# Edge bias written by ScalarE and fewer groups in the tail, in a five-layer graph network on one core

## The chip, the cores and the metric

The kernel runs on one core of one Trainium2 chip. The metric is the device time of one execution in microseconds (us), as the median of several runs. Nothing is sharded, and no other core is used. PE is TensorE, DVE is VectorE, ACT is ScalarE, POOL is GpSimd, SP is SyncE.

## The reference

There are 12500 nodes with 64 features and 200000 edges with 32 attributes, sorted by destination. The destinations are dense at low node numbers (12500 times the square of a uniform number), the sources are uniform. Five layers run one after another:

```
h   = leaky(x @ W1 + b1) @ W2 + b2              # per node
e   = leaky(edge_attr @ We1 + be1) @ We2 + be2  # per edge, leaky slope 0.1
msg = h[src] * e * dot_scale                    # per edge
agg = segment_sum(msg, dst)                     # per node
out = x + agg * res_w
x   = layernorm(out) * ln_g + ln_b
```

Before the layers x is normalized and passed through a relu, and at the end the input is added. All is in float32. The change touches how `be2` is added to `e` and when a group of edges is worked on.

## The kernel before

The kernel is written engine by engine, each with its own program, ordered by semaphores alone. The first 1150 to 1240 us sort edges and prepare tables; they are not touched.

A layer then has two kinds of edge work. The first 101376 edges (dense destinations) lie in *slot groups*: 126 groups of 1024 slots, whose source rows are fetched in blocks and picked by a one-hot product on PE (`gathered`, line 1053, into `slot_ps`). The other edges lie in *gathered groups*: 97 groups of up to 1024 edges and one spill group (number 6), 98 in all. GpSimd fetches their source rows from `h_rows` by indirect DMA, 128 rows each (line 793), into a ring of nine buffers.

The loop has one slot group per step, 126 steps. Gathered groups are spread over them: `a_before(s)` counts the groups before step s, `a_at(s)` is the group whose message is made in step s, if any, and `b_at(s)` is the slot group. Before the change 92 gathered groups lie in the loop and six in the *tail*, six steps (126 to 131) with one group each. A chunk is 14 slot groups that add to the same nodes; the nine chunks have windows of 360, 328, 288, 248, 208, 168, 128, 88 and 48 columns, in this order.

In step s, each engine in its own order:

- PE: first edge product (`hidden_of`, line 976) for the groups of step s + 2, both kinds, into `hid_ps`; after the message of this step, the second edge product (`edge_out`, line 980) of the next gathered group into `e_ps`; after the slot message, that of the next slot group into `slot_ps`; window sums of this step's group (line 1016), which share a bank with the first `hid_ps` and so wait for the leaky operation of group s + 2; chunk sums (line 1029); then `gathered` for the next slot group (line 1053), which overwrites `slot_ps` once its contents were copied to `slot_e`.
- ACT: `hidden_tenth` (line 1252), 0.1 times the first product plus bias, for both kinds of step s + 2.
- DVE: the message product of the gathered group (line 1764, `msg_ready`), the slot product (line 1771, `slot_msg_ready`), the one-hot of the next group (line 1684), the leaky operation of both groups of step s + 2 (line 1676, `hid_acted`), the bias addition from `slot_ps` to `slot_e` and that within `e_ps` (line 1680), the addition of this step's window sums to the nodes (line 1732), then the one-hot for the next slot group (line 1684, up to 2880 columns).
- SP: after the message, the source indices of the group nine later (`load_src`), then attributes, picks and rows of later steps.

Node tiles (14 of 896 nodes) are finished as soon as all their edges are in. Each has a set of parts (`tile_parts`) hung into the middle or end of steps: centering, square, variance, root (line 1201), reciprocal (line 1618), affine (lines 1289 and 1291), then the two products of the next layer's h and its bias (line 1646, h_out). Eleven tiles lie in the loop, every ninth step, two in the tail (three steps each), and the last one follows in two pieces. The next layer's gathers wait until every tile's h is stored.

Of the kernel before, what the change touches and what calls it, by code (L numbers as in the profile page):

```python
# [11 lines left out]
P = 128  # L12
# [24 lines left out]
SPILL_AT = 6  # L37
# [7 lines left out]
TAIL_STEPS = 3  # L45
RECORD_BUFS = 6
# [23 lines left out]
def build(nc, a, N, D, E, ED, L):  # L70
# [19 lines left out]
    IN_LOOP = GA - TAIL_SLOTS * TAIL_STEPS  # L90
# [5 lines left out]
    def a_before(s):  # L96

        return -(-max(s, 0) * IN_LOOP // NB) if s <= NB else min(IN_LOOP + s - NB, GA)

# [48 lines left out]
    with ExitStack() as ctx:  # L148
# [187 lines left out]
        e_biased, slot_e_biased = sem("e_biased"), sem("slot_e_biased")  # L336
# [491 lines left out]
        def _(pe):  # L828
# [149 lines left out]
            def edge_out(acts, to):  # L978
                for j in range(TPH):
                    mm = pe.matmul(to[:, j * P:(j + 1) * P], acts[:, j * TILE:(j + 1) * TILE],  # L980
                                   w2s[:, :], start=True, stop=True)
                return mm

            def far_pass(l):
                with pe.Fori(0, NG) as g:
# [4 lines left out]
                    edge_out(hidden[:, 0, 0, :], e_ps).then_inc(far_e_ready, 1)  # L990
# [10 lines left out]
            def edges(l, last):  # L1001
                pe.wait_ge(edge_w_landed, 16 * (l + 1))
                pe.wait_ge(w2s_ready, 3 * (l + 1))
                pe.wait_ge(h_biased, 2 * (l + 1) * NT)
                own_wait(pe, "pe")

# [39 lines left out]
                def gathered(i):  # L1046
                    pe.wait_ge(source_pick_landed[i % 2], 16 * (l * (NB // 2) + i // 2 + 1))
                    pe.wait_ge(source_rows_landed[i % 2], 16 * (l * (NB // 2) + i // 2 + 1))
                    for k in range(TPG):
                        side, j = k % 2, k // 2  # L1050
                        for half in range(2):
# [3 lines left out]
                                           source_rows[0:ROWS, i % 2, k * D:(k + 1) * D], start=True, stop=True)  # L1055
# [3 lines left out]
                def step(s, part):  # L1059
# [15 lines left out]
                    if now == SPILL_AT:  # L1075
                        pe.wait_ge(spill_msg_ready, l + 1)
                    elif now is not None:
                        pe.wait_ge(msg_ready, l * GR + real(now) + 1)
                    if m is not None:
                        pe.wait_ge(hid_acted[0], l * GA + m + 1)  # L1080
                        edge_out(hidden[:, 0, m % 2, :], e_ps).then_inc(e_ready, 1)
                    k = b_at(s)
                    if k is not None:
                        pe.wait_ge(slot_msg_ready, l * NB + k + 1)
                    k = b_at(s + 1)
                    if k is not None:
                        pe.wait_ge(hid_acted[1], l * NB + k + 1)
                        edge_out(hidden[:, 1, k % 2, :], slot_ps).then_inc(slot_e_ready, 1)
                    if now is not None and now != SPILL_AT:
                        pe.wait_ge(hid_acted[0], l * GA + a_before(s + 3))  # L1090
                        window_sums(now)
                    if b_at(s) is not None:
                        if k is None:
                            own_wait(pe, "pe")
                        chunk_sums(s)
                    part("middle")
                    if k is not None:
                        pe.wait_ge(slot_e_biased, l * NB + k + 1)
# [91 lines left out]
        def _(act):  # L1190
# [68 lines left out]
            def edges(l, last):  # L1259
                k = l + 1  # L1260
                act.wait_ge(w2s_ready, 3 * (l + 1))
                own_wait(act, "act")

                def step(s, part):
# [667 lines left out]
```

## Time and profile before

| | |
|---|---|
| median of 3 runs | 6477.07 us (6475.02 to 6480.55) |
| profiled execution | 6486.53 us |
| its span | 6484.7 us |
| PE, PE loads busy | 5552.7 us (86%), 3637.9 us (56%) |
| DVE busy | 5172.2 us (80%) |
| ACT busy | 1136.5 us (18%) |
| POOL busy | 4526.1 us (70%) |
| mean granted TensorE clock | 0.886 |
| first gather, first message product of layer 1 | 1154.4, 1244.0 us |
| last layer: message product of step 126 | 6421.34 us |

The times in the rows are counted from the start of the span. The third layer serves as the model: its gathers begin at 3354.0 us, its loop is from 3371 to 4326, its tail to 4386, and the next layer's gathers begin at 4414.55. A one-hot or a product that starts less than 0.1 us ahead of the end of its predecessor on the same engine is pipelined with it.

### The profile page before, as it was taken

How to read it: one execution, taken by the hardware profiler on the slowest of the kernel's cores; microseconds unless marked ns; L12 is line 12 of the kernel's file. 1: busy time of each engine (PE TensorE's matmuls, PEld its weight loads, DVE VectorE, ACT ScalarE, POOL GpSimd, SP SyncE). 2: the span in 40 equal slices, each digit the busy share in tenths (PEclk: the TensorE clock that was granted, in tenths of full speed). 3: DMA queues.
4: the chain of work that ended last, by engine and by line, in shares of the span. 5: the costliest groups of instructions: out<-in, count | busy, mean ns of one | idle time of the engine just before them, and what ended most of it. 6: DMA issues, size and time to landing. Idle time of an engine off the chain costs nothing.

```text
span 6484.7 us, 169144 instructions
## 1 busy us (share of the span) xinstructions
PE 5552.7 (86%) x63332; PEld 3637.9 (56%) x63333; DVE 5172.2 (80%) x7991; ACT 1136.5 (18%) x1726; POOL 4526.1 (70%) x4793
## 2 busy tenths in 40 slices
PE   6776899988888788988878898888898887888887
PEld 2222444456666555666645666655566664556665
DVE  8997644598888678888759888867888885998886
ACT  0000311111222211122211122221112222111111
POOL 5777777766777367777737777755777773777776
PEclk9998555699999789999979999988999997999997
DMA  3111299755566345556635555644555663556664
GB/s 138 26 26 44 60 245 244 196 139 141 144 151 162 100 123 135 154 144 162 160 79 136 145 150 150 163 119 111 132 154 146 154 166 76 138 150 155 160 176 112
DMA packets 733545, 886.20 MB, mean 137 GB/s; under 512 B 325488, under 2 KB 502976, under 8 KB 731568
## 3 DMA queue, kind: packets, MB, share of 16 engines
q1 hardware_dynamic: 568480, 703.64, 41.1%
q0 software_dynamic: 152144, 154.93, 11.3%
q10 hardware_dynamic: 12096, 16.53, 0.7%
q8 instruction: 530, 8.68, 0.6%
q14 instruction: 295, 2.42, 0.1%
HBM read 749.51 MB, written 125.06 MB: 135 GB/s over the span
## 4 chain that ended last, share of the span: by engine, by line
PE 59%; DVE 21%; issue 13%; DVEq 4%; ACT 2%; DMA 1%; POOL 0%; SPq 0%; ACTq 0%; POOLq 0%
PE bank L980 15%; PE bank L1029 10%; PE bank L1053 7%; PE bank L976 6%; PE bank L922 4%; PE bank L1016 4%; PE bank L879 3%; DVE arena L1764 3%; PE bank L860 2%; DVE arena L1676 2%; PE bank L845 2%; DVE arena L1422 2%; DVE arena L1684 2%; DVE x_packed L1684 2%; PE bank L901 2%
## 5 line engine op out<-in xcount | busy, mean ns | idle before, releaser
L793 POOL DMA_INDIRECT arena<-h_rows,src x3855 | 3673.0, 953 | 1588.7 <-issue 1252.5
L980 PEld LDWEIGHTS bank<-w2s,arena 128*128 128x128 f32 x8960 | 1154.8, 207 | 945.8 <-DVE arena L1764 600.7
L980 PE MATMUL bank<-w2s,arena 128*128 128x128 f32 x8960 | 1288.8, 299 | 393.6 <-DVE arena L1764 331.4
L780 POOL DMA_INDIRECT slots<-arena,slot_index x792 | 787.4, 994 | 267.2 <-issue 241.6
L1053 PEld LDWEIGHTS bank<-arena 112*64 112x64 f32 x20160 | 643.9, 138 | 288.5 <-issue 268.5
L1053 PE MATMUL bank<-arena 112*64 112x64 f32 x20160 | 729.5, 226 | 59.8 <-issue 54.3
L976 PE MATMUL bank<-x_packed,edge_w 64*128 64x512 f32 x1260 | 718.8, 651 | 1.3 <-DMA x_packed<-slot_attr 1.2
L1252 ACT ACTIVATE arena<-bank,tenth 128x512 f32<-128x512 f32 x490 | 335.5, 685 | 2159.5 <-PE bank L976 2159.5
L976 PE MATMUL bank<-nodes_state,edge_w 64*128 64x512 f32 x980 | 581.6, 675 | 113.0 <-DVE nodes_state L1745 65.6
L1684 DVE TENSOR_TENSOR arena<-bank,slot_rel 128x2880 f32<-128x2880 f32 (+8 forms) x315 | 592.4, 1881 | 51.0 <-issue 44.7
L1684 DVE TENSOR_TENSOR x_packed<-bank,slot_rel 128x2880 f32<-128x2880 f32 (+8 forms) x315 | 592.1, 1880 | 48.9 <-issue 42.3
L1252 ACT ACTIVATE x_packed<-bank,tenth 128x512 f32<-128x512 f32 x630 | 430.0, 683 | 683.3 <-PE bank L976 683.3
L1680 DVE TENSOR_TENSOR arena<-bank,b2s 128x512 f32<-128x512 f32 x630 | 433.0, 687 | 129.4 <-PE bank L980 126.2
L1676 DVE SCALAR_TENSOR_TENSOR arena<-bank,edge_w,arena 128x512 f32<-128x512 f32 x490 | 366.1, 747 | 210.1 <-ACT arena L1252 207.2
L1029 PE MATMUL bank<-arena 64*64 64x288 f32 (+8 forms) x10080 | 531.0, 350 | 0.0
L1029 PE MATMUL bank<-x_packed,arena 64*64 64x288 f32 (+8 forms) x10080 | 529.2, 349 | 0.0
L1676 DVE SCALAR_TENSOR_TENSOR arena<-bank,edge_w,x_packed 128x512 f32<-128x512 f32 x630 | 468.3, 743 | 17.6 <-ACT x_packed L1252 16.6
L1771 DVE TENSOR_TENSOR arena<-arena,bank 128x512 f32<-128x512 f32 x630 | 429.2, 681 | 28.0 <-PE bank L1053 25.6
L1732 DVE TENSOR_TENSOR nodes_state<-nodes_state,bank 64x80 f32 x970 | 227.2, 234 | 273.5 <-PE bank L1016 121.4
L1016 PE MATMUL bank<-arena 128*64 128x80 f32 x7760 | 410.5, 253 | 20.5 <-DVE arena L1676 13.6
L1684 DVE TENSOR_TENSOR arena<-bank,rel 128x640 f32<-128x640 f32 x485 | 396.8, 818 | 0.0
L1029 PEld LDWEIGHTS bank<-arena 64*64 64x64 f32 x10080 | 316.1, 138 | 130.4 <-issue 9.2
(198 smaller groups left out, 5702.0 us busy)
## 6 DMA issues: line engine op xcount, KB each, us to landing
arena<-slot_pick SPq DMA_DIRECT2D x630, 448.0 KB
arena<-h_rows SPq DMA_DIRECT2D x630, 224.0 KB
x_packed<-slot_attr SPq DMA_DIRECT2D x630, 128.0 KB
nodes_state<-attr_t SPq DMA_DIRECT2D x485, 128.0 KB
arena<-h_rows,src POOLq DMA_INDIRECT x3855
slot_pick<-arena SPq DMA_DIRECT2D x126, 448.0 KB
x_packed<-slots SPq DMA_DIRECT2D x127, 136.0 KB, 4.8
slots<-arena SPq DMA_DIRECT2D x9, 1904.0 KB, 22.2
```

Source lines behind the costliest of these rows:

```text
L780: pool.indirect_dma_start(slots, bass.IndirectOffsetOnAxis(ap=slot_index[:, t:t + 1], axis=0), records[:, v, j, :], None).then_inc(record_ ...
L793: pool.indirect_dma_start(to[0:n, at:at + D], None, table, bass.IndirectOffsetOnAxis(ap=index[0:n, t:t + 1], axis=0)).then_inc(landed(t), 16)
L976: return pe.matmul(hid_ps[k][:, :], edge_w[rows_of, 0:P], attributes, start=True, stop=True)
L980: mm = pe.matmul(to[:, j * P:(j + 1) * P], acts[:, j * TILE:(j + 1) * TILE], w2s[:, :], start=True, stop=True)
L1016: mm = pe.matmul(win_ps[side * D:(side + 1) * D, 0:WIN], msg[:, 0, at:at + D], pick[:, k % 2, side * TPH + j, :], start=(j == 0), stop=(j ...
L1029: mm = pe.matmul(sum_ps[half][side * D:(side + 1) * D, 0:w], msg[slots_of, 1, at:at + D], slot_places[i % 2][slots_of, k * w:(k + 1) * w], ...
L1053: mm = pe.matmul(slot_ps[half * D:(half + 1) * D, k * D:(k + 1) * D], source_pick[0:ROWS, i % 2, slot:slot + D], source_rows[0:ROWS, i % 2 ...
L1252: return act.activation(hid_tenth[k], hid_ps[k][:, :], ACT.Identity, scale=SLOPE, bias=tenth[:, :])
L1676: return dve.scalar_tensor_tensor(out, hid_ps[k][:, :], edge_w[:, 2 * P + D:2 * P + D + 1], hid_tenth[k], ALU.add, ALU.max)
L1680: return dve.tensor_tensor(out.rearrange("p (t f) -> p t f", f=D), of.rearrange("p (t f) -> p t f", f=D), b2s[:, :].unsqueeze(1).to_broadc ...
L1684: return dve.tensor_tensor(out, column_ps[:, 0:n].unsqueeze(1).to_broadcast((P, tiles, n)), where.unsqueeze(2).to_broadcast((P, tiles, n)) ...
L1771: dve.tensor_tensor(msg[:, 1, :], slot_e, slot_ps[:, :], ALU.mult).then_inc(slot_msg_ready, 1)
```

## The change

`TAIL_GROUPS = 3` takes the place of six: 95 groups lie in the loop, and the tail has its groups in steps 126, 128 and 130. The second edge bias leaves DVE. ScalarE writes `b2s` into the bank `e_ps` once the message that read it is made, and into `slot_ps` once the slot message is made, and PE's second edge product adds onto it (`start=False`). ScalarE also copies `slot_ps` to `slot_e`, and DVE multiplies with `e_ps` as soon as PE is done. PE writes both banks once at the head of a layer with eight small products, so that later ones may add. In PE's program the wait for the message moves from ahead of the edge products to ahead of the window sums, and that for the slot message to ahead of the chunk sums.

```diff
-    IN_LOOP = GA - TAIL_SLOTS * TAIL_STEPS
+    IN_LOOP = GA - TAIL_GROUPS
-        return -(-max(s, 0) * IN_LOOP // NB) if s <= NB else min(IN_LOOP + s - NB, GA)
+        return -(-max(s, 0) * IN_LOOP // NB) if s <= NB else min(IN_LOOP + (s - NB + 1) // 2, GA)
@@ PE
-            def edge_out(acts, to):
+            def edge_out(acts, to, onto_bias):
                 for j in range(TPH):
                     mm = pe.matmul(to[:, j * P:(j + 1) * P], acts[:, j * TILE:(j + 1) * TILE],
-                                   w2s[:, :], start=True, stop=True)
+                                   w2s[:, :], start=not onto_bias, stop=True, skip_group_check=onto_bias)
@@ PE, head of a layer
+                for to in (e_ps, slot_ps):
+                    for j in range(TPH):
+                        mm = pe.matmul(to[:, j * P:(j + 1) * P], ident[:, :], ones[:, :], start=(j == 0), stop=True,
+                                       skip_group_check=True)
+                mm.then_inc(banks_written, 1)
@@ PE, step
-                    if now == SPILL_AT:
-                        pe.wait_ge(spill_msg_ready, l + 1)
-                    elif now is not None:
-                        pe.wait_ge(msg_ready, l * GR + real(now) + 1)
                     if m is not None:
                         pe.wait_ge(hid_acted[0], l * GA + m + 1)
-                        edge_out(hidden[:, 0, m % 2, :], e_ps).then_inc(e_ready, 1)
-                    k = b_at(s)
-                    if k is not None:
-                        pe.wait_ge(slot_msg_ready, l * NB + k + 1)
+                        pe.wait_ge(e_begun, l * GA + m + 1)
+                        edge_out(hidden[:, 0, m % 2, :], e_ps, True).then_inc(e_ready, 1)
                     k = b_at(s + 1)
                     if k is not None:
                         pe.wait_ge(hid_acted[1], l * NB + k + 1)
-                        edge_out(hidden[:, 1, k % 2, :], slot_ps).then_inc(slot_e_ready, 1)
+                        pe.wait_ge(slot_e_begun, l * NB + k + 1)
+                        edge_out(hidden[:, 1, k % 2, :], slot_ps, True).then_inc(slot_e_ready, 1)
                     if now is not None and now != SPILL_AT:
+                        pe.wait_ge(msg_ready, l * GR + real(now) + 1)
                         pe.wait_ge(hid_acted[0], l * GA + a_before(s + 3))
                         window_sums(now)
                     if b_at(s) is not None:
+                        pe.wait_ge(slot_msg_ready, l * NB + s + 1)
                         chunk_sums(s)
                     part("middle")
                     if k is not None:
-                        pe.wait_ge(slot_e_biased, l * NB + k + 1)
+                        pe.wait_ge(slot_e_kept, l * NB + k + 1)
                         gathered(k)
@@ ACT, step
+                def bias(to):
+                    return act.activation(to[:, :].rearrange("p (t f) -> p t f", f=D),
+                                          b2s[:, :].unsqueeze(1).to_broadcast((P, TPG, D)), ACT.Identity)
...
+                    now, m = a_at(s), a_at(s + 1)
+                    if now == SPILL_AT:
+                        act.wait_ge(spill_msg_ready, l + 1)
+                    elif now is not None:
+                        act.wait_ge(msg_ready, l * GR + real(now) + 1)
+                    if m is not None:
+                        bias(e_ps).then_inc(e_begun, 1)
+                    i = b_at(s)
+                    if i is not None:
+                        act.wait_ge(slot_msg_ready, l * NB + i + 1)
+                    i = b_at(s + 1)
+                    if i is not None:
+                        bias(slot_ps).then_inc(slot_e_begun, 1)
                     for side, n, k in ((0, GA, a_at(s + 2)), (1, NB, b_at(s + 2))):
                         if k is not None:
                             act.wait_ge(hid_ready[side], l * n + k + 1)
                             hidden_tenth(side).then_inc(tenth_ready[side], 1)
+                    if i is not None:
+                        act.wait_ge(slot_e_ready, l * NB + i + 1)
+                        act.activation(slot_e, slot_ps[:, :], ACT.Identity).then_inc(slot_e_kept, 1)
                     part("middle")
@@ DVE, step
-                        dve.wait_ge(e_biased, l * GA + k + 1)
+                        dve.wait_ge(e_ready, l * GA + k + 1)
...
-                        dve.wait_ge(slot_e_biased, l * NB + i + 1)
+                        dve.wait_ge(slot_e_kept, l * NB + i + 1)
...
-                    if i is not None:
-                        dve.wait_ge(slot_e_ready, l * NB + i + 1)
-                        edge_biased(slot_e, slot_ps[:, :]).then_inc(slot_e_biased, 1)
-                    if m is not None:
-                        dve.wait_ge(e_ready, l * GA + m + 1)
-                        edge_biased(e_ps[:, :], e_ps[:, :]).then_inc(e_biased, 1)
```

## Rows read from the trace of the kernel before

**Rows 1.** Busy time by stretch: loop, tail and last chunk of the third layer (start:end, length, engines, PE clock)
```profile
3371.00:4326.00 955.00, 853.15 (x11933) 610.42 (x11934) 823.80 (x1147) 186.03 (x280) 723.61 (x760) 0.97 0.59 150
4326.00:4386.00 60.00, 37.34 (x204) 22.47 (x204) 27.92 (x44) 10.24 (x15) 2.83 (x4) 0.67 0.08 23
4238.00:4326.00 88.00, 78.83 (x1261) 60.10 (x1260) 68.56 (x119) 20.09 (x30) 66.81 (x70) 0.96 0.66 166
```

**Rows 2.** Timeline of DVE in a full step of the first chunk (start, duration, engine, line)
```profile
3401.62 0.68 DVE L1764 TENSOR_TENSOR arena<-arena,bank 128x512 f32<-128x512 f32 x1
3402.22 0.68 DVE L1771 TENSOR_TENSOR arena<-arena,bank 128x512 f32<-128x512 f32 x1
...
3403.55 0.74 DVE L1676 SCALAR_TENSOR_TENSOR arena<-bank,edge_w,arena 128x512 f32<-128x512 f32 x1
...
3404.86 0.68 DVE L1680 TENSOR_TENSOR arena<-bank,b2s 128x512 f32<-128x512 f32 x1
...
3406.06 0.59 DVE L1732 TENSOR_TENSOR nodes_state<-nodes_state,bank 64x80 f32 x2
...
3409.75 0.68 DVE L1764 TENSOR_TENSOR arena<-arena,bank 128x512 f32<-128x512 f32 x1
```

**Rows 3.** Timeline of PE in the same step
```profile
3402.35 2.05 PE L980 MATMUL bank<-w2s,arena 128*128 128x128 f32 x16 [0.79 <-DVE arena L1764]
3404.34 0.77 PE L1016 MATMUL bank<-arena 128*64 128x80 f32 x16
```

**Rows 4.** Waits in the loop of the third layer (total us, times, longest)
```profile
PE bank L980 <- DVE arena L1764: 61.4, 51, 4.8
```

**Rows 5.** Timeline of DVE in a step whose successor has no group
```profile
3506.38 0.68 DVE L1771 TENSOR_TENSOR arena<-arena,bank 128x512 f32<-128x512 f32 x1
...
3508.33 0.69 DVE L1680 TENSOR_TENSOR arena<-bank,b2s 128x512 f32<-128x512 f32 x1
3509.88 0.60 DVE L1732 TENSOR_TENSOR nodes_state<-nodes_state,bank 64x80 f32 x2 [0.85 <-PE bank L1016]
```

**Rows 6.** First and last gather, a landing in the chain, use of the last loop group
```profile
3353.99 0.95 POOL L793 DMA_INDIRECT arena<-h_rows,src  x1 [86.41 <-issue]
...
4319.06 0.68 DVE L1764 TENSOR_TENSOR arena<-arena,bank 128x512 f32<-128x512 f32 x1
...
4328.84 0.91 POOL L793 DMA_INDIRECT arena<-h_rows,src  x1 [0.30 <-issue]
...
5507.99 4.52 DMA arena<-h_rows,src
```

**Rows 7.** Bias additions in the loop, by form (count, busy, mean ns, idle before)
```profile
L1680 DVE TENSOR_TENSOR arena<-bank,b2s 128x512 f32<-128x512 f32 x125 | 85.9, 687 | 22.3 <-PE bank L980 21.8 <-issue 0.2
L1680 DVE TENSOR_TENSOR bank<-bank,b2s 128x512 f32<-128x512 f32 x91 | 62.8, 691 | 0.0
```

**Rows 8.** Timeline of ACT: the nearest operations to the new ones
```profile
3402.18 0.68 ACT L1252 ACTIVATE x_packed<-bank,tenth 128x512 f32<-128x512 f32 x1
...
4351.32 0.76 ACT L1289 ACTIVATE nodes_state<-normed,ln_w 64x448 f32 x1 [7.43 <-DVE normed L1623]
...
4358.50 1.03 ACT L1207 ACTIVATE y_sum<-bank,node_w 128x448 f32<-128x448 f32 x1 [2.69 <-PE bank L845]
...
4372.77 0.54 ACT L1196 ACTIVATE square<-bank 128x448 f32<-128x448 f32 x1 [7.22 <-PE bank L833]
```

**Rows 9.** Timeline of the tail: first root, both reciprocals, first message, last h_out
```profile
4329.40 0.69 DVE L1764 TENSOR_TENSOR arena<-arena,bank 128x512 f32<-128x512 f32 x1
...
4340.00 0.63 ACT L1201 ACTIVATE std<-bank,eps 128x448 f32<-128x448 f32 x1 [2.08 <-PE bank L838]
...
4347.50 2.95 DVE L1618 RECIPROCAL rstd<-std 128x448 f32<-128x448 f32 x1
...
4380.77 2.95 DVE L1618 RECIPROCAL rstd<-std 128x448 f32<-128x448 f32 x1
...
4395.58 0.69 DVE L1646 TENSOR_TENSOR h_out<-bank,node_w 112x512 f32<-112x512 f32 x1 [2.85 <-PE bank L860]
```

More of the change, by code:

```diff
@@ L45 @@
 TAIL_STEPS = 3
+TAIL_GROUPS = 3
 RECORD_BUFS = 6
@@ L989, in far_pass @@
                     pe.wait_ge(far_hid_acted, n + 1)
-                    edge_out(hidden[:, 0, 0, :], e_ps).then_inc(far_e_ready, 1)
+                    edge_out(hidden[:, 0, 0, :], e_ps, False).then_inc(far_e_ready, 1)
                     with pe.Fori(0, FW) as w:
@@ L1054, in gathered @@
                                            source_pick[0:ROWS, i % 2, slot:slot + D],
-                                           source_rows[0:ROWS, i % 2, k * D:(k + 1) * D], start=True, stop=True)
+                                           source_rows[0:ROWS, i % 2, k * D:(k + 1) * D], start=(k == 0), stop=True,
+                                           skip_group_check=True)
                             if k == TPG - 1:
@@ L1092, in step @@
                     if b_at(s) is not None:
-                        if k is None:
-                            own_wait(pe, "pe")
+                        pe.wait_ge(slot_msg_ready, l * NB + s + 1)
+                        own_wait(pe, "pe")
                         chunk_sums(s)
@@ L1261, in edges @@
                 act.wait_ge(w2s_ready, 3 * (l + 1))
+                act.wait_ge(banks_written, l + 1)
                 own_wait(act, "act")
+                def bias(to):
+                    return act.activation(to[:, :].rearrange("p (t f) -> p t f", f=D),
+                                          b2s[:, :].unsqueeze(1).to_broadcast((P, TPG, D)), ACT.Identity)
                 def step(s, part):
+                    now, m = a_at(s), a_at(s + 1)
[5 more added lines that the diff above has]
+                        bias(e_ps).then_inc(e_begun, 1)
+                    elif now is not None:
+                        own_wait(act, "act")
+                    i = b_at(s)
[4 more added lines that the diff above has]
+                        bias(slot_ps).then_inc(slot_e_begun, 1)
+                    elif b_at(s) is not None:
+                        own_wait(act, "act")
                     for side, n, k in ((0, GA, a_at(s + 2)), (1, NB, b_at(s + 2))):
```

3 lines of the change are left out of this document (2 added, 1 removed).

## The prediction

> **What bounds the kernel now.** I read the stretches first, then the waits, then the queues of single steps in order of time. The third layer is the model: its first gather starts at 3354.0, the next layer's at 4414.5, so a layer lasts 1060.5 us. Inside it lie the 126 steps of the loop (955 us), the six steps of the tail (60 us) and the hand-over to the next layer (45 us) [rows 1]. In the loop PE is busy 89% and DVE 86% of the time. Neither share tells the bound; the order of the work does.
>
> Take one step of the first chunk that has a gathered group and prepares another [rows 2]. I count from the start of the slot product S (3402.22); the group product M starts 0.60 before it, at -0.60, and ends at 0.08. DVE then runs back to back: S, one-hot of the group, two leaky operations, two bias additions (2.64 to 3.93), window additions at 3.84, one-hot of the slot group at 4.46, next M. The step takes 8.13, and no gap is left on DVE. PE meanwhile stood idle 0.79 for M, ran both second edge products in 2.05 from 0.13, and had the window sums done at 2.89 [rows 3]. So this step is bound by DVE, but with little to spare: the window sums were ready 0.95 before DVE reached their addition. Over the layer's loop PE waited 61 us for M in this way, 51 times [rows 4].
>
> A step whose successor has no group has one bias addition only [rows 5]: counted from S at 3506.38, the one edge product starts at 0.79, the bias addition at 1.95, the window additions at 3.50. There DVE idles 0.85.
>
> The last chunks differ: PE is busy 79 of 88 us and DVE 69 [rows 1]; the slot one-hot is short there, and PE's own queue is nearly as long as the step.
>
> The gathers are the floor. GpSimd starts the first of the layer's 776 at 3353.99 and the last at 4328.84, one every 1.258 us, so it is not held back; a gather lands 4.52 us after its start [rows 6]. The 92nd group, the last of the loop, ends with gather 733: it lands at 4279 and is used at 4319.06, 40 us later. Gathers don't bind yet.
>
> **The change, part by part.**
>
> (a) DVE loses both bias additions in each step: 0.69 each, 125 and 91 of them in this loop, 149 us in busy time [rows 7].
>
> (b) ScalarE gets an operation that writes the bias into the bank before PE adds to it. The trace has no such operation. The nearest rows are 0.68 for the 512-column one in the loop, 0.76 for 448 columns read from SBUF; the ends are 0.54 and 1.03 [rows 8]. I take 0.72. Each 0.1 more costs about 0.1 in each of the 95 group steps, so the ends are worth -85 and +145 us over five layers. A hand-over from DVE to ScalarE takes 0.14 (normed ends 4351.18, next starts 4351.32) [rows 8]; from M to PE it took 0.05 [rows 2, 3]. From ScalarE to PE I take 0.1.
>
> By the Trainium skill (VectorE: DVE Perf Modes, The TRN2 errata) a ScalarE operation that reads SBUF has 52 cycles of 1.2 GHz more fixed time than one that reads PSUM; that makes an estimate of 0.73 out of the 0.68 measured in the loop [rows 8], and the sum would stay. No row here shows this very operation.
>
> (c) The path of the step is then: M ends 0.08, bias into e_ps 0.22 to 0.94, edge products from 1.04 to 3.09, window sums to 3.8, window additions at the earliest 4.1. More important is the order of ScalarE's queue: the bias into slot_ps waits for the end of S, and both 0.1x operations (hidden_tenth) are queued behind it. They ran from -0.62 to 0.64 before [rows 8]; now the slot bias runs 0.84 to 1.56, the 0.1x operations end at 2.15 and 2.75, and DVE's leaky operations, which began at 1.33, begin at 2.17 and 2.8. DVE's window additions came 1.55 after the start of the last operation ahead of them in the half-filled step [rows 5], the time its sequencer took for loading the window starts; so they come at 4.25. That is 0.40 later than 3.84. The freed 1.28 us of DVE become idle time ahead of the leaky operations.
>
> The four kinds of step, start of S to window additions or one-hot, before and after:
> - group now, next and after next: 3.84 to 4.25, +0.40
> - group now and next, none after next (S at 3410.34): one leaky less, so the PE path decides: 3.77 to 4.1, +0.33
> - group now, none next: 3.49 to 4.27, +0.78, because the slot product now waits for the bias and the leaky operations behind it
> - none now (S at 3432.73): no window additions; the one-hot moves from 3.84 to 3.47, -0.37.
>
> They follow each other about once in four steps: +1.14 in four, 0.285 a step. In the first six chunks (84 steps) that is +24 us. In the last three PE's queue already covers most of the detour, since its hidden products end after S; I take 0.07 a step, +3.
>
> (d) The copy of slot_e on ScalarE (0.69) begins at about 3.1 and ends by 3.8; chunk sums cover it in wide chunks, and in the last ones it replaces a DVE operation that ended no earlier. Nothing. If chunk sums were gone it would cost up to 0.7 a step.
>
> (e) Node tiles in the loop: ScalarE's biased and squared operations now stand ahead of the bias that PE waits for. One such place per tile (1.03 [rows 8]) is partly covered: 0.4 a tile, 11 tiles, +4.
>
> (f) Three more groups in the loop. After the change, from S to the next S and without the one-hot's length, the four kinds take 5.45, 5.30, 4.90 and 4.05 (the places above, plus 0.6 for window additions where there are any and 0.6 for M where the next step has one), 4.93 in the mean. A loop of full steps alone would have 0.52 more for a quarter more groups, so one group costs 2.1: +6 a layer.
>
> (g) The tail. Now it runs from M at 4329.40 to the second tile's h_out, ending 4396.27: 66.9 us for its two tiles. The first std ends at 4340.63, but its reciprocal starts at 4347.50, behind one group's hidden product, edge product, bias and sums; the second std ends at 4376.02, its reciprocal starts at 4380.77 [rows 9]. With a group in every other step the first reciprocal follows at once (-6.9, +1 given back by the group of the next step), and the second waits for window sums alone (-2.5) with one group less ahead of its centering (-3.4). Sum -12. In the last layer no h is made, the last window is added ahead of the last reciprocal, and the final pieces need not wait for it: -18 out of the 63 us from M at 6421.34 to the end.
>
> (h) Eight small products at the head of the layer write the banks once (some 3 us on PE, as 16 such records take 2.05 to 3.5). The first long one-hot on DVE covers them. Nothing; without cover +3 a layer.
>
> (i) Waits that move: ScalarE now waits for M and S, with all its later work behind them (priced in c). PE's wait for M moves to the window sums. SyncE's and GpSimd's queues keep their order; SyncE's source load still follows M.
>
> Sum: +37 for the loop in four layers, +34 in the last, which has fewer tile operations; less 12 and 18. 4 x 25 + 16 = +116 us. The profiled execution took 6486.5 around a span of 6484.7, 9.5 above the median of 6477.1; I add the change to the median: 6593.
>
> **The rivals.**
> Rival 1, faster: the loop is really DVE's. Its place is DVE between one-hot and the leaky operations: if the 0.1x operations are done by then, the 1.28 us come off every full step. It decides in favour of faster once the detour on ScalarE costs less than 0.9 of them. For it: DVE back to back in [rows 2]. Against it: the queue order on ScalarE. The gain is capped by gathers: 95 groups are 757 gathers, 952 us, and land by 955 after the layer's first, against 965 for the use of the last group now: -10 a layer, -12 for the tail. The first layer's gathers start 90 us early, so it may gain 42; the last pays for groups that land later, +3. Sum -105: 6372. The Trainium skill (Perfetto Trace Analysis, Optimizing Scalar/DVE Operations) says that moving work to Scalar may make sense when DVE is saturated; [rows 2] show it saturated, so by that page it would come out this way. Chance 0.14.
>
> Rival 2, a little faster: detour and relief cancel; what is left is +6 for the groups and the tail: 30 - 66 = -36, 6441. For it: the bare DVE-to-window path differs by only 0.3 to 0.4 in most steps. Chance 0.14.
>
> Rival 3, much slower: the bias costs nearer 1.0, tile steps pay in full, and PE, idle more, falls to its lower clock. It was granted 0.97 over this loop and 0.67 in the tail [rows 1]. The loop grows by 60: 5 x 60 - 66 = +234, 6711. Chance 0.12.
>
> **How the numbers follow.** The forecast has 0.60, with its own range 6500 to 6670. For 8 in 10 the range is 6430 to 6690: it takes in rival 2 and leaves out rival 1 and the outer half of rival 3. Within 0.2% (13 us) is what a measurement of this kernel can't tell from no change. Faster: rival 1 and most of rival 2, 0.25. Same: 0.06. Slower: 0.69.
>
> **What would show it.** Right: a full step of the first chunk takes 8.4 to 8.6, with DVE idle some 0.8 ahead of the first leaky and ScalarE's new operation between M and the edge products; a step without a successor grows by 0.7; the tail is 12 shorter; gathers end long before they are used. Wrong: leaky operations still at 1.4 after S, DVE waiting for landings, a tail of unchanged length, or a bias operation under 0.6 or above 0.9.

## The result, and the profile after the change

The changed kernel takes 6554.01 us (median of 4 runs, 6550.88 to 6559.46), the one before 6478.81 on the same chip. The ratio is 1.011, with a 95% interval of 1.0096 to 1.0125: 75 us slower, where 116 were predicted. The profiled execution took 6555.08 us around a span of 6553.2, 68.5 more than the span of before. A repetition (changed_again, below) gave 1.0112 (1.0087 to 1.0137). On two of the four chips of the experiments every kernel, that of before included, took 11.0 to 11.8 ms at a granted clock of 0.70 to 0.72; results from there are marked (slow chip), are compared only with runs of before on the same chip, and carry little on small terms.

The page of the kernel after, engines and the groups that the prediction speaks of (L1270 is the new bias operation, L1297 the copy to `slot_e`, L1705 the leaky operation):

```profile
PE 5532.8 (84%) x63412; PEld 3635.4 (55%) x63413; DVE 4520.7 (69%) x6871; ACT 2106.7 (32%) x3476; POOL 4524.4 (69%) x4793
L1270 ACT ACTIVATE bank<-b2s 128x512 f32<-128x512 f32 x1120 | 670.7, 604 | 1960.2 <-DVE arena L1800 984.3
L1705 DVE SCALAR_TENSOR_TENSOR arena<-bank,edge_w,arena 128x512 f32<-128x512 f32 x490 | 368.0, 751 | 503.8 <-ACT arena L1256 502.7
```

DVE is rid of 652 us of work, and the kernel is slower. The idle time ahead of DVE's leaky operations of the gathered groups, ended by ScalarE, is more than twice what it was (502.7 against 207.2 us). The same stretches of the third layer as in [rows 1]:

```profile
3404.40:4389.70 985.30, 858.34 (x12012) 613.84 (x12013) 705.52 (x944) 380.26 (x628) 727.32 (x763) 0.97 0.61 146
4389.70:4451.00 61.30, 38.68 (x173) 22.91 (x173) 19.66 (x29) 12.09 (x18) 0.00 (x0) 0.55 0.07 20
```

The loop (first slot product to the last) was 954.0 and is 985.3. A full step of the first chunk, DVE, PE and ACT (of the kind of [rows 2, 3], three steps earlier; M is L1793, S L1800, the window additions L1761):

```profile
3413.24 0.68 DVE L1793 TENSOR_TENSOR arena<-arena,bank 128x512 f32<-128x512 f32 x1
3413.83 0.68 DVE L1800 TENSOR_TENSOR arena<-arena,bank 128x512 f32<-128x512 f32 x1
...
3415.79 0.75 DVE L1705 SCALAR_TENSOR_TENSOR arena<-bank,edge_w,arena 128x512 f32<-128x512 f32 x1 [0.54 <-ACT arena L1256]
3416.46 0.74 DVE L1705 SCALAR_TENSOR_TENSOR arena<-bank,edge_w,x_packed 128x512 f32<-128x512 f32 x1
3417.93 0.60 DVE L1761 TENSOR_TENSOR nodes_state<-nodes_state,bank 64x80 f32 x2 [0.73 <-PE bank L1023]
```

```profile
3414.70 2.02 PE L981 MATMUL bank<-w2s,arena 128*128 128x128 f32 x16 [1.10 <-ACT bank L1270]
3416.65 0.77 PE L1023 MATMUL bank<-arena 128*64 128x80 f32 x16
```

```profile
3413.95 1.20 ACT L1270 ACTIVATE bank<-b2s 128x512 f32<-128x512 f32 x2 [5.15 <-DVE arena L1793]
3415.09 0.67 ACT L1256 ACTIVATE arena<-bank,tenth 128x512 f32<-128x512 f32 x1
3415.66 0.68 ACT L1256 ACTIVATE x_packed<-bank,tenth 128x512 f32<-128x512 f32 x1
3416.75 0.60 ACT L1297 ACTIVATE arena<-bank 128x512 f32<-128x512 f32 x1 [0.42 <-PE bank L981]
```

The order of events is the one predicted. M ends 0.09 after S starts, ScalarE writes both biases and only then does its 0.1x operations; the leaky operations begin 1.96 after S, not 1.33, and PE starts 0.87 after S, not 0.13. But a bias takes 0.604 us, not 0.72, and it starts 0.03 after M ends, not 0.14: the window additions stand at 4.10 (forecast 4.25, before 3.84).

The tail of the third layer, both reciprocals and the last h_out:

```profile
4405.02 2.95 DVE L1647 RECIPROCAL rstd<-std 128x448 f32<-128x448 f32 x1 [4.88 <-ACT std L1205]
...
4432.91 2.95 DVE L1647 RECIPROCAL rstd<-std 128x448 f32<-128x448 f32 x1
...
4447.71 0.69 DVE L1675 TENSOR_TENSOR h_out<-bank,node_w 112x512 f32<-112x512 f32 x1 [2.85 <-PE bank L861]
```

The first reciprocal follows its root (std ends 4404.92); before, it started 6.9 after the root's end [rows 9]. From the last slot product to the next layer's first gather it is 77.0 us, before 89.6.

### The profile page after: what moved, and what is told of

Same layout as the page of the kernel before. It is cut to its first block, busy times and chain, and to the rows that moved or that the text cites. A ratio compares the mean times of both kernels' runs of the same rounds, so it can differ in the third digit from the quotient of the medians.

```text
span 6553.2 us, 171522 instructions
## 1 busy us (share of the span) xinstructions
PE 5532.8 (84%) x63412; PEld 3635.4 (55%) x63413; DVE 4520.7 (69%) x6871; ACT 2106.7 (32%) x3476; POOL 4524.4 (69%) x4793
## 4 chain that ended last, share of the span: by engine, by line
PE 43%; DVE 19%; issue 16%; POOL 12%; ACT 6%; DVEq 3%; DMA 1%; ACTq 0%; SPq 0%; POOLq 0%
POOL arena L794 11%; PE bank L981 9%; PE bank L1036 7%; PE bank L1060 4%; PE bank L923 4%; PE bank L1023 4%; PE bank L880 3%; ACT bank L1270 3%; PE bank L846 2%; PE bank L861 2%; DVE arena L1713 2%; DVE arena L1793 2%; ACT arena L1256 2%; PE bank L977 2%; DVE x_packed L1713 2%
## 5 line engine op out<-in xcount | busy, mean ns | idle before, releaser
L981 PEld LDWEIGHTS bank<-w2s,arena 128*128 128x128 f32 x8960 | 1140.5, 205 | 1027.1 <-issue 1026.1
L981 PE MATMUL bank<-w2s,arena 128*128 128x128 f32 x8960 | 1261.7, 296 | 509.5 <-ACT bank L1270 505.2
L1270 ACT ACTIVATE bank<-b2s 128x512 f32<-128x512 f32 x1120 | 670.7, 604 | 1960.2 <-DVE arena L1800 984.3
L1705 DVE SCALAR_TENSOR_TENSOR arena<-bank,edge_w,arena 128x512 f32<-128x512 f32 x490 | 368.0, 751 | 503.8 <-ACT arena L1256 502.7
L1761 DVE TENSOR_TENSOR nodes_state<-nodes_state,bank 64x80 f32 x970 | 228.0, 235 | 602.4 <-PE bank L1023 500.8
L977 PE MATMUL bank<-nodes_state,edge_w 64*128 64x512 f32 x980 | 563.1, 655 | 62.5 <-DVE nodes_state L1774 50.4
L1705 DVE SCALAR_TENSOR_TENSOR arena<-bank,edge_w,x_packed 128x512 f32<-128x512 f32 x630 | 469.1, 745 | 115.1 <-ACT x_packed L1256 114.4
L1297 ACT ACTIVATE arena<-bank 128x512 f32<-128x512 f32 x630 | 376.4, 597 | 404.9 <-PE bank L981 377.8
L1800 DVE TENSOR_TENSOR arena<-arena,bank 128x512 f32<-128x512 f32 x630 | 429.8, 682 | 84.8 <-PE bank L1060 74.6
L1023 PE MATMUL bank<-arena 128*64 128x80 f32 x7760 | 403.3, 250 | 48.4 <-DVE arena L1705 42.9
L1023 PEld LDWEIGHTS bank<-arena 128*64 128x64 f32 x7760 | 322.9, 145 | 136.6 <-DVE arena L1705 63.1
```

Of the source, the lines that this page charges most:

```text
L977: return pe.matmul(hid_ps[k][:, :], edge_w[rows_of, 0:P], attributes, start=True, stop=True)
L1023: mm = pe.matmul(win_ps[side * D:(side + 1) * D, 0:WIN], msg[:, 0, at:at + D], pick[:, k % 2, side * TPH + j, :], start=(j == 0), stop=(j ...
L1270: return act.activation(to[:, :].rearrange("p (t f) -> p t f", f=D), b2s[:, :].unsqueeze(1).to_broadcast((P, TPG, D)), ACT.Identity)
L1705: return dve.scalar_tensor_tensor(out, hid_ps[k][:, :], edge_w[:, 2 * P + D:2 * P + D + 1], hid_tenth[k], ALU.add, ALU.max)
L1800: dve.tensor_tensor(msg[:, 1, :], slot_e, slot_ps[:, :], ALU.mult).then_inc(slot_msg_ready, 1)
```

## The experiments

"Loop" is from first to last slot product of a layer, "tail" from there to the next layer's first gather, or to the end. All ratios are to runs of before on the same chip.

**Each part alone.** tail_alone and tail_again are the same kernel, the one before with the new tail:

```diff
-    IN_LOOP = GA - TAIL_SLOTS * TAIL_STEPS
+    IN_LOOP = GA - TAIL_GROUPS
...
-        return -(-max(s, 0) * IN_LOOP // NB) if s <= NB else min(IN_LOOP + s - NB, GA)
+        return -(-max(s, 0) * IN_LOOP // NB) if s <= NB else min(IN_LOOP + (s - NB + 1) // 2, GA)
```

> Only the tail part of the change: 95 groups in the loop, three in the tail; both bias additions stay on DVE as before. The theory of the prediction: the loop grows by 6 us a layer for three more groups (2.1 each), the tail shrinks by 12 to 13 in four layers and by 20 in the last, so 30 - 70 = -40 us: 6439. Rival (the tail's gain needs the relief of DVE, since the bias additions stand between root and reciprocal): the tail shrinks by 6 or less and the loop's 30 us eat it: 6470 to 6490.

> Only the bias part: ScalarE writes the bias into both banks and copies slot_e, six groups stay in the tail. The theory: each layer's loop is 24 us longer than before and the tail hardly changes, so about +110 us on before: 6590. Rival (the bias move is neutral, and it is the three groups more in the loop that cost): no change, 6480.

Measured (slow chip): tail alone 1.0001 (0.9981 to 1.002), bias alone (the changed kernel with the tail of before) 1.0152 (1.0099 to 1.0204). The sign of the second is as expected. The first shows no gain there, not even one of 30 us, which would be a ratio of 0.9973. bias_alone was not repeated elsewhere.

> The tail part alone once more. Theory as before: -12 us a layer in the tail, -20 in the last layer, +6 a layer in the loop, -40 us where the kernel before takes 6477 us. Rival: no gain without the relief of DVE.

> The changed kernel once more, as the reference for the edits of it, since the time of the kernel before in the study's first runs (11205 us) is far from its 6477 us. If what slows these runs is the same for both kernels and independent of the change, the difference stays +75 us (ratio 1.007 at 11200); if it acts through the longer chain between ScalarE and the others, each hand-over costs more and the ratio is 1.011 or more.

Measured: tail_again 6452.74 us, ratio 0.9957 (0.9941 to 0.9973), faster than both kernels; changed_again 6554.51, ratio 1.0112. So the bias costs 102 us on top of the tail, and the tail alone gives 30 where 40 were expected. By layer, in the profiled execution, in us:

```
                 loop, layers 1 to 5                  tail, layers 1 to 5
before           956.9  956.4  954.0  959.1  924.5    90.0  90.0  89.6  89.3  67.7
tail_again       956.8  956.4  958.5  956.4  947.0    80.3  78.3  80.2  80.5  50.5
after            985.7  985.9  985.3  988.3  948.1    77.0  77.2  77.0  73.8  47.5
group_bias_only  991.6  990.2  993.4  996.3  946.5    78.1  77.4  78.3  76.8  49.1
slot_bias_only   978.9  988.8  989.7  985.8  947.3    77.6  80.9  80.9  80.4  50.4
sums_again      1019.0 1013.1 1022.7 1020.2  972.1    77.0  77.3  77.3  76.8  47.4
```

Two things stand out. Three more groups in the loop cost the first four layers nothing (mean +0.4, predicted +6). The last layer's loop grew by 22.5 from the groups alone, and then by only 1.1 from the bias. There the message waits for its rows. The rows show the waits of the message product and the last message of that loop, in tail_again and after, and for after the landing of its last rows (from `--critical`):

```profile
DVE arena L1765 <- DMA arena<-h_rows,src: 21.5, 14, 3.7
6388.28 0.69 DVE L1765 TENSOR_TENSOR arena<-arena,bank 128x512 f32<-128x512 f32 x1 [3.70 <-DMA arena<-h_rows,src]
```

```profile
DVE arena L1793 <- DMA arena<-h_rows,src: 9.2, 5, 4.1
6495.71 2.42 DMA arena<-h_rows,src
6498.23 0.69 DVE L1793 TENSOR_TENSOR arena<-arena,bank 128x512 f32<-128x512 f32 x1 [0.94 <-DMA arena<-h_rows,src]
```

This is the gathers' floor. After the change the layer's first gather starts at 5545.0 and the 757th, the last that the loop needs, at 6495.71; its message is made as soon as it has landed, 953.2 us after the first gather. In tail_again, where the layer's gathers begin at 5434.97, it is 953.3. The four kernels of the table with 95 groups in the loop and the sums in their old place lie within 1.6 us of each other there (946.5 to 948.1), whatever their bias does.

**One bias only.** Both keep the new tail. group_bias_only leaves the slot bias on DVE, slot_bias_only the group bias:

```diff
-                        edge_out(hidden[:, 1, k % 2, :], slot_ps, True).then_inc(slot_e_ready, 1)
+                        edge_out(hidden[:, 1, k % 2, :], slot_ps, False).then_inc(slot_e_ready, 1)
...
+                        edge_biased(slot_e, slot_ps[:, :]).then_inc(slot_e_kept, 1)
```

```diff
-                        edge_out(hidden[:, 0, m % 2, :], e_ps, True).then_inc(e_ready, 1)
+                        edge_out(hidden[:, 0, m % 2, :], e_ps, False).then_inc(e_ready, 1)
...
+                        edge_biased(e_ps[:, :], e_ps[:, :]).then_inc(e_biased, 1)
```

> Three tail groups; only the gathered groups' bias goes to ScalarE, the slot group's stays on DVE (edge product with start, bias addition into slot_e). Theory: ScalarE's queue has no wait for S, so the leaky operations are early again, but the slot's edge product ends at 2.9 and its bias addition stands ahead of the window additions: 4.4 in full steps (4.09 in the changed kernel), 3.5 in steps without a successor (4.08), one-hot at 3.35 in steps without a group (3.28). Sum near that of the changed kernel, 6540 to 6610. Rival (the wait for S is all of the cost): 6450 to 6480.

> Three tail groups; only the slot group's bias and copy go to ScalarE, the gathered groups' bias addition stays on DVE. Theory: PE starts the group's edge product 0.06 after M again, but the leaky operations stay at 1.95 and the bias addition follows them: window additions at 4.1 in full steps, 3.55 where there is no group after next, 4.08 without a successor; one-hot at 3.85 without a group. 6530 to 6600. Rival (ScalarE's operation between M and the edge product is all of the cost): 6450 to 6480.

Measured: 6586.76, ratio 1.0159 (1.0135 to 1.0184), and 6559.80, ratio 1.0118 (1.0095 to 1.0141), both in their ranges. Either bias alone costs at least as much as both: +134 and +107 us over tail_again, against +102. DVE in a full step of group_bias_only, then of slot_bias_only (window additions last):

```profile
3426.80 0.68 DVE L1789 TENSOR_TENSOR arena<-arena,bank 128x512 f32<-128x512 f32 x1
...
3429.72 0.69 DVE L1698 TENSOR_TENSOR arena<-bank,b2s 128x512 f32<-128x512 f32 x1 [0.16 <-PE bank L981]
3431.28 0.60 DVE L1750 TENSOR_TENSOR nodes_state<-nodes_state,bank 64x80 f32 x2 [0.87 <-issue]
```

```profile
3411.11 0.68 DVE L1794 TENSOR_TENSOR arena<-arena,bank 128x512 f32<-128x512 f32 x1
...
3413.06 0.75 DVE L1699 SCALAR_TENSOR_TENSOR arena<-bank,edge_w,arena 128x512 f32<-128x512 f32 x1 [0.54 <-ACT arena L1259]
...
3414.39 0.69 DVE L1703 TENSOR_TENSOR bank<-bank,b2s 128x512 f32<-128x512 f32 x1
3415.20 0.60 DVE L1755 TENSOR_TENSOR nodes_state<-nodes_state,bank 64x80 f32 x2
```

With the group's bias on ScalarE alone, PE starts late but DVE still has to wait for PE to add the slot's bias, and the window additions come at 4.48, later than before or after the change. With the slot's alone they come at 4.09, as with both: the group's bias on DVE (L1703) lies wholly in the idle time that stands ahead of the window additions after the change, and costs nothing in such a step.

**Is DVE the bound?** idle_filled and idle_again are the changed kernel with one more 0.68 us operation per step on DVE, ahead of the leaky operations:

```diff
+                        dve.wait_ge(extra_done, l * NB + i)
+                        dve.tensor_tensor(extra[:, :].rearrange("p (t f) -> p t f", f=D),
+                                          column_ps[:, :].rearrange("p (t f) -> p t f", f=D),
+                                          b2s[:, :].unsqueeze(1).to_broadcast((P, TPG, D)), ALU.add).then_inc(extra_done, 1)
```

> The changed kernel with one more DVE operation per slot step (0.69 us, a bias addition into an array that nobody reads, 630 in all) between the group's one-hot and the leaky operations, where DVE now sits idle 0.55. It adds work and leaves nothing out. The theory (the step follows the path message, bias, edge products, window sums; the freed DVE time is idle time ahead of the leaky operations): 0.05 to 0.15 a step, +30 to +90 us on the changed kernel. Rival (DVE's own work still sets the step): 630 x 0.6 = +380 us.

> The changed kernel with one more DVE operation (0.69 us, into an array nobody reads) per slot step, in the idle time ahead of the leaky operations; a second try at the usual times. Theory: idle time is filled, +30 to +90 us on the changed kernel's 6554. Rival (DVE's work sets the step): +380 us.

Measured: 1.0068 (1.0041 to 1.0094, slow chip), and 6561.96 us, ratio 1.0124 (1.0102 to 1.0146). The rows of the added operation:

```profile
L1808 DVE TENSOR_TENSOR extra<-bank,b2s 128x512 f32<-128x512 f32 x630 | 429.5, 682 | 0.0
```

430 us more work on DVE cost 7 us by the medians, about the spread of such runs and less than the 30 to 90 expected. The profiled executions show more: the five loops of idle_again are 27 us longer than after the change (4920.5 against 4893.3), and its first loop starts 18 us earlier, which hides most of it. Either number is far below 380. After the change DVE is not the bound.

**The order of ScalarE's and PE's queues.** tenths_first moves ScalarE's 0.1x operations between the two bias operations. sums_first and sums_again do that too, and put PE's window sums ahead of the slot group's second edge product:

```diff
+                    if now is not None and now != SPILL_AT:
+                        pe.wait_ge(msg_ready, l * GR + real(now) + 1)
+                        pe.wait_ge(hid_acted[0], l * GA + a_before(s + 3))
+                        window_sums(now)
                     k = b_at(s + 1)
                     if k is not None:
                         pe.wait_ge(hid_acted[1], l * NB + k + 1)
...
```

> The changed kernel with one edit in ScalarE's queue: both 0.1x operations stand ahead of the wait for the slot product and of the bias into slot_ps. The theory of one path (message, bias, two edge products, window sums, window additions, one-hot): in full steps the slot edge product now waits for a later bias, 2.5 us after S and not 1.4, so window sums come 0.45 later there; in the steps without a group now or next it gains 0.3 to 1.0; in all about the time of the changed kernel, 6540 to 6570. Rival (the late leaky operations alone are what costs): 0.4 to 0.6 a step come back, 6554 - 300 = 6250 without the gathers' floor and about 6400 with it.

> As tenths_first, and PE does the window sums ahead of the slot group's edge product, so that they wait for the message, one bias, one edge product and the early leaky operation alone. The theory: window additions at 3.5 us after S in a full step (4.1 in the changed kernel, 3.84 before); the loops of layers 2 to 5 then run into the gathers (the 95th group lands 955 us after the layer's first gather), which caps the gain: about 6390, faster than both kernels. Rival (DVE's relief is worth nothing, PE or ScalarE bounds the step by its own work): 6500 or more.

> The changed kernel with ScalarE's 0.1x operations ahead of its wait for the slot product, and PE's window sums ahead of the slot group's edge product; a second try beside a kernel before that takes 6483 us. The first try's undisturbed steps have the window additions 3.76 after S in full steps (4.09 in the changed kernel, 3.84 before) and 3.1 to 3.8 in steps without a successor (4.08, 3.50), but the slot's edge product at 1.84 in steps without a group now (0.59). The theory of one path: loop 0.3 to 0.5 a step shorter than in the changed kernel, 40 to 60 us a layer where the gathers allow it (10 below the kernel before), so 6390. Rival (the slot group has a path of its own, slot product, bias, edge product, copy, gathered, which this edit makes longer): 6500 or more, no gain on the changed kernel.

Measured: tenths_first 1.0518 (1.0473 to 1.0563, slow chip), sums_first 1.0314 (1.0274 to 1.0355, slow chip), sums_again 6707.52 us, ratio 1.0354 (1.0318 to 1.039). My theory failed here. The window additions do come earlier, at 3.76 in the median undisturbed full step, and yet a layer's loop is 24 to 37 us longer than after the change. The waits of S for the gathered product and of the window sums (L1023) for the leaky operation, after and in sums_again, and a step of sums_again whose successor has no group (DVE, then PE and ScalarE's slot bias):

```profile
DVE arena L1800 <- PE bank L1060: 74.6, 89, 2.9
PE bank L1023 <- DVE arena L1705: 42.9, 147, 1.9
```

```profile
DVE arena L1800 <- PE bank L1060: 365.3, 331, 3.5
PE bank L1023 <- DVE arena L1705: 323.8, 318, 5.6
3489.61 0.68 DVE L1800 TENSOR_TENSOR arena<-arena,bank 128x512 f32<-128x512 f32 x1
3490.61 0.75 DVE L1705 SCALAR_TENSOR_TENSOR arena<-bank,edge_w,arena 128x512 f32<-128x512 f32 x1 [0.32 <-ACT arena L1256]
...
3498.71 0.69 DVE L1800 TENSOR_TENSOR arena<-arena,bank 128x512 f32<-128x512 f32 x1 [2.19 <-PE bank L1060]
```

```profile
3491.41 0.78 PE L1023 MATMUL bank<-arena 128*64 128x80 f32 x16 [2.24 <-DVE arena L1705]
3492.12 2.01 PE L981 MATMUL bank<-w2s,arena 128*128 128x128 f32 x8
3494.05 3.40 PE L1036 MATMUL bank<-x_packed,arena 64*64 64x360 f32 x32
3497.39 1.15 PE L1060 MATMUL bank<-arena 112*64 112x64 f32 x32
3491.04 0.60 ACT L1270 ACTIVATE bank<-b2s 128x512 f32<-128x512 f32 x1
```

The sums wait for the leaky operation, since they share its bank, and now the slot group's edge product, chunk sums and gathered product stand behind them: PE idles 2.24, the slot group's edge product starts 2.5 after S instead of 1.46, and the next S waits 2.19. Of that delay of 1.05 the sums are the last 0.5 only: the slot's bias, now behind both 0.1x operations, ends 2.03 after S. The same rows show slow products: eight take 2.01, where they took 1.16 in a busy stretch, and 32 chunk sums 3.40 instead of 2.65; the granted clock from 3492.0 to 3498.7 was 0.75. So there are two paths round the step, as the rival on record for sums_again has it, and I had priced one. What each of the two edits costs is open: tenths_first ran on a slow chip alone, and there ScalarE's order by itself cost more than with the sums moved too.

**The last layer with six tail groups.**

```diff
+        if in_last[0]:
+            n = GA - TAIL_SLOTS * TAIL_STEPS
+            return -(-max(s, 0) * n // NB) if s <= NB else min(n + s - NB, GA)
...
```

> The kernel before with three tail groups in the first four layers and six in the last one; the edge bias stays on DVE. With three tail groups in every layer the loop (first to last slot product) kept its length in four layers (956.8, 956.4, 958.5, 956.4 us against 956.9, 956.4, 954.0, 959.1 before) and grew from 924.5 to 947.0 in the last, while the rest of that layer fell from 67.7 to 50.5. Theory: the last layer, which has the shortest steps, is then held by the landing of its gathers (95 groups land 24 gathers, some 30 us, after 92); so with six there its loop is back at 924 to 926 and its rest at 67 to 68, which is 5 us less for that layer than with three: 6441 in the span, about 6448 where the kernel before has 6483, ratio 0.9948. Rival: three more groups cost the last layer its own work in DVE and PE; then the loop is shorter by only 3 x 2.1 us and the time is 10 to 15 us above that, ratio 0.997.

Measured: 11013.84 us, ratio 0.9998 (0.9973 to 1.0023), slow chip: unsettled. Whether it beats tail_again stays open.

## Why the prediction was right, and where only its sum was

The sign holds, and so does the main claim that the order of work sets the time, not DVE's share: (a) came out in full and brought nothing, and idle_again excludes rival 1. Where in the loop the time is lost came out otherwise. Rival 2 (6441) falls too; the "bare path" did cancel in clean steps, but not in tile steps. Rival 3's bias of 1.0 fell with the row of L1270.

Most of the loop's sum is a coincidence. Mean growth per layer over the first four, by the place of the step in its tile's nine (step number modulo 9; tile work stands in places 0 to 5), in us:

```
                     wide chunks (steps 18 to 83)       last chunks (84 to 124)
                     tail_again    after   steps        tail_again    after   steps
places 6, 7, 8           +0.8      -0.2    21             -2.5       -2.5    14
place 0                   0.0      +2.0     8             +0.1       +1.0     4
place 1                  -0.3      +3.1     8             +1.0       +4.7     4
place 2 (reciprocal)     +1.2      -3.4     8             -0.1       -2.4     4
places 3, 4, 5           +0.9     +17.0    21             +0.9       +8.8    15
steps 0 to 17            -1.6      +1.7
```

**(b), (c)** The four offsets from S became 4.09, 3.85, 4.08 and (one-hot) 3.28 in the median undisturbed step, against 4.25, 4.1, 4.27 and 3.47 forecast. (The step at 3432.73, from which the fourth was read before, is the spill group's; steps without any group have the same 3.84.) Their changes are +0.25, +0.07, +0.58 and -0.57: +0.08 a step, not 0.285. The terms that failed are the bias operation (0.60, not 0.72) and the hand-over (0.03, not 0.14). Steps without tile work are no longer than before: the +24 and +3 of (c) are about zero.

**(e)** The tiles, priced at +4, carry all of it: places 0 to 5 grow by 18.7 and 12.0, 2.6 to 2.7 for each tile. The mechanism that (e) names is there: ScalarE's own tile work stands ahead of the bias that PE waits for. Here is the step after the affine operation, ACT and PE after the change, with S at 3671.68, then PE in the same step of tail_again, with S at 3605.14:

```profile
3672.47 1.02 ACT L1211 ACTIVATE y_sum<-bank,node_w 128x448 f32<-128x448 f32 x1 [3.96 <-PE bank L846]
3673.28 0.69 ACT L1270 ACTIVATE bank<-b2s 128x512 f32<-128x512 f32 x1
```

```profile
3674.11 1.13 PE L981 MATMUL bank<-w2s,arena 128*128 128x128 f32 x8 [0.89 <-ACT bank L1270]
```

```profile
3605.92 1.13 PE L981 MATMUL bank<-w2s,arena 128*128 128x128 f32 x8
```

The edge product starts 2.43 after S, where it started 0.78 after S with the bias on DVE; the step takes 9.36 instead of 7.81, and the granted clock was 1.00 in both.

Slow products are seen in tiles too: PE idles around the 2.95 us reciprocal, and the granted clock of the next step is down. But they are there without the bias. The same step before, in tail_again and after (PE's edge products; the stretch from S to the next S, whose third number from the end is the granted clock):

```profile
3621.64 3.00 PE L980 MATMUL bank<-w2s,arena 128*128 128x128 f32 x16 [3.53 <-issue]
3621.50:3630.00 8.50, 8.36 (x99) 6.48 (x100) 7.63 (x12) 1.15 (x2) 6.62 (x7) 0.80 0.24 60
```

```profile
3596.05 3.79 PE L981 MATMUL bank<-w2s,arena 128*128 128x128 f32 x16 [4.12 <-DVE arena L1765]
3595.90:3605.10 9.20, 9.05 (x101) 7.31 (x102) 6.88 (x10) 1.24 (x3) 7.07 (x8) 0.76 0.25 46
```

```profile
3662.69 3.76 PE L981 MATMUL bank<-w2s,arena 128*128 128x128 f32 x16 [4.62 <-ACT bank L1270]
3661.80:3671.70 9.90, 9.01 (x98) 7.27 (x99) 5.76 (x9) 3.80 (x6) 7.46 (x9) 0.66 0.20 42
```

The step takes 8.44, 9.23 and 9.85. More than half of its growth comes with the three groups more in the loop, by which another kind of step falls on this place, and so do the slow products (3.79 in tail_again, 3.76 after); the bias adds 0.5 of idle time.

Over the whole program the division is plain. PE's second edge products, their mean time in ns and PE's idle time ahead of them, before, in tail_again and after, and the loop of the third layer in tail_again (behind the length stands PE's busy time; the same stretch after the change is shown in the section on the result):

```profile
L980 PE MATMUL bank<-w2s,arena 128*128 128x128 f32 x8960 | 1288.8, 299 | 393.6 <-DVE arena L1764 331.4
```

```profile
L981 PE MATMUL bank<-w2s,arena 128*128 128x128 f32 x8960 | 1264.4, 297 | 408.1 <-DVE arena L1765 361.5
3343.10:4301.60 958.50, 856.78 (x12010) 615.61 (x12011) 832.83 (x1163) 187.67 (x282) 726.46 (x762) 0.97 0.62 150
```

```profile
L981 PE MATMUL bank<-w2s,arena 128*128 128x128 f32 x8960 | 1261.7, 296 | 509.5 <-ACT bank L1270 505.2
```

From tail_again to after that loop grew by 26.8. PE's busy time grew by 1.6 of it (856.8 to 858.3) and its idle time by 25.2, at a granted clock of 0.97 in both. The products are not slower (297 and 296 ns); PE waits 101 us longer ahead of them, nearly all of it for the new operation. So the 2.6 a tile are waiting, not clock, and rival 3's lower clock did not come either (0.886 before and 0.890 after over the whole span).

The tiles don't take the same share when one bias moves alone. In places 3 to 5 of the wide chunks slot_bias_only grows by 8.6 and group_bias_only by 8.8, where both together give 17.0; but steps 0 to 17, which have no tile work, grow by 6.7 and 4.7, where both give 1.7.

**Where the 0.72 came from.** I had it from operations with a per-partition bias operand (0.68 for 512 columns) and from 0.76 for 448 read from SBUF. The plain row of the same group, 0.54 for the 448 columns of the square, was the right one: ScalarE's plain copy of 512 columns, which reads PSUM and writes SBUF, takes 0.597 after the change:

```profile
L1297 ACT ACTIVATE arena<-bank 128x512 f32<-128x512 f32 x630 | 376.4, 597 | 404.9 <-PE bank L981 377.8
```

The bias operation reads SBUF and writes PSUM in 0.604. The Trainium skill (VectorE: DVE Perf Modes, The TRN2 errata) charges ScalarE 52 cycles of 1.2 GHz more for reading SBUF, an estimate of 0.043 us; here it is 0.007 with the other destination. The Trainium skill (ScalarE: Activation LUTs, Step-by-step: what each stage is for) calls PSUM the faster destination, which could hide the rest; no run here has the two apart.

**(d), (h)** cost nothing visible: the copy of `slot_e` at 3416.75 ends at 3417.35, where the chunk sums begin, and steps 0 to 17 together grow by 1.7. PE's gathered product waited for the copy five times in the whole program, 3.4 us in all, after the change and in sums_again alike.

**(f)** was wrong in both halves. Three groups more cost 0.4 us in the first four layers, not 6, and 22.5 in the last. The forecast had laid the gathers' floor beside a loop of the inner layers and not beside the shortest: in the last layer the last slot product of the loop stood 938 us after the first gather (5479.1 to 6417.0), and 757 gathers and the last landing take 953. Rival 1 alone allowed for it: its -105 comes out only if its +3 is the whole last layer, the tail's -18 included, which leaves +21 for that loop. The 4.52 us for a landing was one case; the one that holds the last loop after the change took 2.42.

**(g)** The tail came out at -12.6 in the third layer (forecast -12) and -20.2 in the last (-18). By tail_again, 9.7, 11.7, 9.4, 8.8 and 17.2 of the five layers' gain are the groups'; 1 to 7 a layer are the bias's. (g) let the first reciprocal follow its root by the groups alone. It doesn't: in the third layer of tail_again it starts 2.83 after the root ends (4317.21 to 4320.04), behind a bias addition on DVE, and only with the bias on ScalarE does that fall to 0.10.

**The sum.** Loops +142 (forecast +182), tails -74 (-66): 68 of the 68.5 us. Of the 40 missing in the loops, 22 are (f) in four layers, 10 the last layer, held by its gathers, and 7 the bias in four layers, where 31 a layer were forecast and 29.3 came (after less tail_again). That this last term is so close is luck: (c) was forecast at 27 and gave about nothing, (e) at 4 and gave nearly all.

## What to carry to other kernels

A share of busy time doesn't say what a moved operation is worth: DVE fell from 80% to 69% and the kernel became slower, because the work went into a queue whose later operations another engine was waiting for. Price such a move on its worst steps, here those with node-tile work, and write down every cycle of dependence round the step, not only the one that the change touches. Before work is moved forward in a loop, lay the transfers' floor beside the shortest instance of that loop.

## What the runs showed of the hardware that was not expected

- Plain ScalarE operations on 128x512 took 0.597 (PSUM to SBUF) and 0.604 us (SBUF to PSUM); with a per-partition bias operand 0.68.
- Window additions started at least 1.46 to 1.56 us after the start of the last operation ahead of them that had to wait, even with their sums done (3429.72 to 3431.28 in group_bias_only, its gap of 0.87 put down to issue). In the step of [rows 5] the two loads of the window starts on DVE's sequencer, 0.30 us each, and what is done with them there take 1.2 of the 1.55 us.
- Indirect gathers of 128 rows started one per 1.26 us (the 757th of the last layer 950.7 us after its first), and landed 2.42 us after their start in one place and 4.52 in another.
